# Graph convolution and FFN layer on one core: in the final masked addition, two node tiles of every seven go from VectorE to ScalarE and GpSimd

## The reference

```python
x = x + gnn(layernorm(x), edge_weight, ..., edge_index, ...)   # two graph convolutions and a linear layer
x = x + ffn(layernorm(x)[None], ...)[0]
```

```python
_, idx = jax.lax.top_k(weights, k)
sel_idx = idx[:, :kk]
y = y * w_sel[..., None]
processed = jnp.zeros_like(x).at[batch_idx, sel_idx].set(y)
return processed + x
```

## Time and profile before

| | before |
|---|---|
| time, median of 3 runs | 2256.4 us (2253.57, 2256.4, 2258.93) |
| profiled execution, from its first to its last instruction | 2757.6 us |
| profiled execution, its own time beside the span | not recorded |
| DVE busy | 892.5 us, 32% |
| ACT busy | 994.1 us, 36% |
| POOL busy | 1559.2 us, 57% |
| PE busy | 1849.8 us, 67% |
| mean granted TensorE clock | 0.836 |

### The profile page before, as it was taken

How to read it: one execution, slowest core, us unless ns; L and a number is a source line. 1 busy time by engine, 2 the same in 40 slices (tenths; PEclk the granted TensorE clock), 3 DMA queues, 4 the chain that set the end, 5 groups by cost and what they waited for, 6 DMA issues and landing times.

```text
span 2757.6 us, 44466 instructions
## 1 busy us (share of the span) xinstructions
PE 1849.8 (67%) x7203; PEld 1470.7 (53%) x7204; DVE 892.5 (32%) x2440; ACT 994.1 (36%) x2506; POOL 1559.2 (57%) x1584
## 2 busy tenths in 40 slices
PE   0366666675666565655687787788877777777781
PEld 0255445454444444443476666666666666665671
DVE  6322222222222222221243343333333333333346
ACT  2333333233233333333333443343434344334440
POOL 1556656665665666666455666565666556565600
PEclk9978887877887778777689999988898888888895
DMA  5523323332333333333222222222222222222202
GB/s 173 155 82 90 88 84 88 88 90 84 93 91 86 89 94 91 92 92 90 73 77 78 80 81 82 78 77 76 80 82 82 76 76 82 78 83 80 82 8 93
DMA packets 138002, 237.44 MB, mean 86 GB/s; under 512 B 57535, under 2 KB 87357, under 8 KB 137984
## 3 DMA queue, kind: packets, MB, share of 16 engines
q0 software_dynamic: 75264, 205.62, 26.1%
q1 hardware_dynamic: 47848, 20.06, 2.7%
q10 hardware_dynamic: 14872, 11.58, 1.3%
HBM read 216.94 MB, written 19.38 MB: 86 GB/s over the span
## 4 chain that ended last, share of the span: by engine, by line
PE 29%; issue 21%; another core or an unknown queue 20%; DVEq 11%; DVE 8%; ACT 4%; POOL 3%; ACTq 2%; DMA 2%; POOLq 0%; SPq 0%
PE ps_agg L537 19%; PE ps_dn L628 4%; PE ps_up L635 3%; POOL ring L309 3%; ACT ring L384 2%; DVEq L820 2%; DVEq L808 2%; DVE acc L816 2%; DVEq L816 1%; DVE S L808 1%; DMA ring<-conv_rows,idx_stage 1%; DVEq L838 1%; ACTq L328 1%; DVEq L815 1%
## 5 line engine op out<-in xcount | busy, mean ns | idle before, releaser
L537 PE MATMUL ps_agg<-ring,S 128*128 128x256 f32 x3136 | 974.7, 467 | 719.0 <-ACT ring L384 392.7
L537 PEld LDWEIGHTS ps_agg<-ring,S 128*128 128x128 f32 x3136 | 715.1, 236 | 915.0 <-issue 792.1
L309 POOL DMA_INDIRECT ring<-conv_rows,idx_stage x784 | 774.7, 988 | 535.2 <-DVEq L837 295.4
L309 POOL DMA_INDIRECT ring<-normed_rows,idx_stage x784 | 775.1, 989 | 494.3 <-issue 263.3
L384 ACT ACTIVATE ring<-ring,wc 128x256 f32<-128x256 f32 x1568 | 669.7, 502 | 76.5 <-issue 41.4
L816 DVE TENSOR_TENSOR acc<-acc,ps_agg x490 | 206.3, 421 | 1179.1 <-remote 635.2
L808 DVE TENSOR_TENSOR S<-iota,dstc 128x512 f32 x392 | 271.8, 693 | 484.7 <-issue 480.9
L537 PE MATMUL ps_agg<-ring,S_more 128*128 128x256 f32 x768 | 202.8, 411 | 31.5 <-DVE S_more L808 27.7
L628 PE MATMUL ps_dn<-fw2s,hT 128*128 128x256 f32 x864 | 217.2, 408 | 0.0
L635 PE MATMUL ps_up<-xnT,fw1s 128*128 128x256 f32 x832 | 196.9, 391 | 1.2 <-ACT hT L447 1.2
L537 PEld LDWEIGHTS ps_agg<-ring,S_more 128*128 128x128 f32 x768 | 158.6, 210 | 69.3 <-issue 44.1
(11 more groups left out here) (165 smaller groups left out, 1072.8 us busy)
## 6 DMA issues: line engine op xcount, KB each, us to landing
ring<-normed_rows,idx_stage POOLq DMA_INDIRECT x784
ring<-conv_rows,idx_stage POOLq DMA_INDIRECT x784
conv_rows<-rows ACTq DMA_DIRECT2D x50, 128.0 KB
out_rows<-xs SPq DMA_DIRECT2D x6, 896.0 KB
xs<-in_x SPq DMA_DIRECT2D x4, 1280.0 KB, 14.4
normed_rows<-acc SPq DMA_DIRECT2D x4, 1280.0 KB, 5.2
idx_stage<-idx SPq DMA_DIRECT2D x200, 4.0 KB
normed_rows<-acc SPq DMA_DIRECT2D x1, 1152.0 KB, 4.8
```

Source lines behind the costliest of these rows:

```text
L309: pool.indirect_dma_start(out=ring[:, k, :], out_offset=None, in_=f_dram if l == 0 else t2_dram, in_offset=bass.IndirectOffsetOnAxis(ap=id ...
L537: last = nc.tensor.matmul(to, select[:, t, :], ring[:, q * TG + t, :], start=(t == 0), stop=(t == TG - 1))
```

## The change

In every chunk of seven tiles DVE keeps the first five. For the last two, ACT multiplies `acc` by the column of `mw`, in place, and then POOL adds both products to both `xs` tiles in one instruction of 128 x 512. ACT starts when DVE signals that `mw` is complete (`mask_ready`). POOL waits for ACT's pair (`ffn_scaled`). SP waits for both halves of a chunk before it issues the DMA. DVE's part shrinks from 49 to 35 instructions; ACT gets 14 and POOL 7.

```diff
+        mask_ready, out_ready_pool = sem("mask_ready"), sem("out_ready_pool")
+        ffn_scaled = sem("ffn_scaled")
+        OUT_POOL = 2
...
             for c, (w0, w1) in enumerate(OUTCH):
                 sp.wait_ge(out_ready, c + 1)
+                sp.wait_ge(out_ready_pool, c + 1)
...
+            for c, (w0, w1) in enumerate(OUTCH):
+                pool.wait_ge(ffn_scaled, c + 1)
+                last = nc.gpsimd.tensor_tensor(xs[:, X0 + w1 - OUT_POOL:X0 + w1, :], acc[:, A0 + w1 - OUT_POOL:A0 + w1, :], xs[:, X0 + w1 - OUT_POOL:X0 + w1, :], op=ALU.add)
+                last.then_inc(out_ready_pool, 1)
...
+            act.wait_ge(mask_ready, 1)
+            act.wait_ge(down_kept, NW + SKEW + 1)
+            act.wait_ge(base_done, NW + SKEW + 1)
+            for c, (w0, w1) in enumerate(OUTCH):
+                for w in range(w1 - OUT_POOL, w1):
+                    last = nc.scalar.activation(acc[:, A0 + w, :], acc[:, A0 + w, :], ACT.Copy, scale=mw[:, w:w + 1])
+                last.then_inc(ffn_scaled, 1)
...
             lk(V.tensor_tensor(mw[:, :], mw[:, :], u, op=ALU.mult))
+            dve.sem_inc(mask_ready, 1)
 
             dve.wait_ge(down_kept, NW + SKEW + 1)
             dve.wait_ge(base_done, NW + SKEW + 1)
             for c, (w0, w1) in enumerate(OUTCH):
-                for w in range(w0, w1):
+                for w in range(w0, w1 - OUT_POOL):
```

## The result

Over six runs each, the changed kernel takes 2266.14 us (2265.39 to 2267.36), the kernel before 2257.66 us. The ratio is 1.0037, with a 95% interval of 1.0024 to 1.0050: slower by 8.5 us (5.4 to 11.3). The forecast was slower, 2262.5 us, in a range from 2254.5 to 2269; the narrower range of the forecast's own case, 2258 to 2265.7, just misses the measured time.

What follows compares the result with a forecast made beforehand. DVE's final additions (19.5 us) and the output DMAs (18.9 us) were taken as balanced in the last stage. Alternation delays chunk 1, moving the data's end from 22.8 to 28.9 us: 2256.4 + 6.1 = 2262.5 us, range 2254.5 to 2269.

Steps and rivals of the forecast that it cites:

- the forecast's own case: Last stage: DVE and POOL take turns at the port; +6.1 us, 2262.5 us, with POOL's addition between 0.5 and 1.55 us.
- the alternation of two engines at one read port: Last stage: one POOL addition, then one DVE tile, 1.5 us a pair; +6.1 us; chance 0.53 together with POOL first.
- T0: Start of DVE's first final addition, from which the last stage is counted; 2731.17 us in the profile of the kernel before.
- the sum: Last stage: chunk 1 ready at 11.7 us, 1.05 to first byte, 16.1 of DMA, less 22.8 before: +6.1 us, or 7P - 1.6.
- The term P: Length of one POOL addition of 128 x 512, taken as 1.1 us, with bounds of 0.5 and 1.55 us.
- The gap in front: Ahead of DVE's first final addition: the extra DVE signal, put with SP's second wait below 0.1 us.
- No hold: Last stage, rival: POOL runs beside DVE, which keeps its 0.4 us pace; -0.5 us, 2255.9 us; chance 0.13.
- DVE keeps the port: Last stage, rival: POOL gets in only after DVE's 35 instructions; +12.2 us, 2268.6 us; chance 0.15.
- A part of the addition held: Last stage, rival: POOL holds the port for only part of its addition; with half, +0.6 us, 2257.0 us; chance 0.14.
- its edge of 0.87: Hold in us at which, if the engines alternate, the loss reaches the +4.5 us (0.2%) that counts as slower.
- POOL keeps the port: Last stage, rival: all seven POOL additions go first; +6.9 us, 2263.3 us; counted with the forecast in its 0.53.
- the release and the next start: DVE frees POOL's read 0.13 us before its end, its successor starts 0.085 us before it; so a waiting POOL comes first.

Runs made afterwards that it cites:

- pool_memset: Changed kernel with POOL's addition replaced by a fill with zeros, which reads nothing; time ratio 1.0002 against the kernel before, stage 0.65 us shorter.
- dve_psum: Changed kernel with DVE's last operand a PSUM tile in place of the xs tile; time ratio 0.9999 against the kernel before, stage 0.80 us shorter.
- pool_paced: Changed kernel with POOL's addition of each chunk waiting for DVE's part of the chunk before; time ratio 1.0010 against the kernel before, stage +1.64 us.
- pool_copy: Changed kernel with POOL's addition replaced by a one-input copy of ACT's product to xs; time ratio 0.9992 against the kernel before, stage +0.64 us.
- pool_one: Changed kernel with one tile of seven for ACT and POOL in place of two; time ratio 1.0014 against the kernel before, stage +2.23 us.
- pool_three: Changed kernel with three tiles of seven for ACT and POOL in place of two; time ratio 1.0026 against the kernel before, stage +7.23 us.

## Why the prediction was right

**The direction and the mechanism.** It forecast slower, from the alternation of two engines at one read port. The stretches show three tiles at full pace, then seven pairs, as written. Tile 5 was to be ready at T0 + 4.2: SP issued chunk 0 at T0 + 4.25, which less the 0.17 us of SP before is T0 + 4.1. POOL was to be done at about T0 + 12: it was at T0 + 10.8. The empty DMA stretch between the first and the second chunk is there, up to T0 + 12.1 where the sum had 12.75. pool_memset and dve_psum show the cause from both sides, since the first leaves POOL without a read and the second DVE without its second SBUF input, and the loss becomes a gain of 0.65 and 0.80 us.

**The sizes.** The term P, taken as 1.1 us, was the length of POOL's addition; what counts is the hold, and it measured 1.0. With it the sum is 7 x 1.0 - 1.6 = +5.4 us. The gap in front, which I had put below 0.1 us, was 0.19: DVE's signal and what it puts between L1035 and L1043 in the chain above. The DMA rate, taken as 333 GB/s, was 340 once the chunks were waiting, which makes the 5.37 MB 0.3 us shorter. Together that is 5.4 + 0.2 - 0.3 = +5.3, as measured, in place of +6.1. The closeness of the price was luck, in that two errors met: the addition without a hold is 1.28 us long, not 1.1, and it holds DVE for 1.0 us and not for its whole length, which no row of before could show. With the true length as the price the sum would have been 7 x 1.28 - 1.6 = +7.4 us. The Trainium skill, "GPSIMD Engine Reference", section "Elementwise — side-by-side cycle accounting", led to 1.12 us as an estimate; starts were 1.22 us apart in dve_psum, where DVE did not hold POOL.

**Carrying the profile over.** I carried the difference over unchanged from an execution that was 501 us longer. The changed kernel bears this out: its stage takes 31.97 us in an execution of 2263.2 us and 31.93 in one of 2756.6. For the kernel before it is inferred, since its profiles are all near 2760 us.

**The rivals.** "No hold" gave -0.5 us and was measured, with the hold removed, as -0.65 to -0.80. "DVE keeps the port" would have had POOL's first addition end at T0 + 15; it ended before T0 + 2.5. "A part of the addition held" was true in the small: 1.0 of 1.28 us, which is above its edge of 0.87. "POOL keeps the port" is out too, because each 1.4 us holds one DVE tile. Reading the release and the next start (0.13 us before the end against 0.085) gave the right order; that these two times are the reason for it was not tested.

**What stays open.** The measured +8.5 us has a lower end of 5.4, and the stage explains 5.3. The repeats gave +9.1 and +5.5 us. If there were a cost ahead of the stage, the other kernels with the same added code should show it. Their ratios as us of the kernel before in the same set, less their stage's difference, leave (in us) +1.2 for pool_memset, +1.1 for pool_paced, -2.9 for pool_copy, +0.5 for dve_psum, +1.7 for pool_one and -0.1 for pool_three: a mean of +0.3 us, each uncertain by about 4 us or more. So nothing shows such a cost, but 2 us of it can't be excluded.

## What to carry to other kernels

Before work is moved from VectorE to GpSimd, look at what each of the two reads from SBUF while they overlap. If VectorE's instructions have two SBUF inputs and GpSimd's reads at all, VectorE stands still for a part of GpSimd's instruction, and that hold has to be set against what VectorE saves: 1.00 against 0.8 us for the addition of two tiles, 0.34 against 0.8 for a copy. The sign is visible beforehand in the stretched instructions where the two engines happen to meet. Look also at what the consumer behind them can take: here the output DMAs needed 18.9 us beside DVE's 19.5, so even free help was worth at most 0.8 us. And an engine that runs ahead of need on a shared resource should be paced: one wait took away 3.7 of the 5.3 us. Smaller output chunks, with all of the work left on VectorE, shortened the stage by 1.15 us.

## What the runs showed of the hardware

- The hold is not the whole of the holding instruction. A GpSimd addition of 512 columns takes 1.28 us where neither engine holds the other (dve_psum) and holds VectorE for 1.00; a copy of 512 columns holds it for 0.34; a fill holds it not at all. The Trainium skill, "SBUF — State Buffer", section "Who interferes with whom", calls the shared pair of ports an exclusive lock and says, in its item on VectorE's two-port modes, that whoever issues first has the pair for the whole instruction. Which instructions contend is in these runs as it says; the hold between an instruction with two SBUF inputs and a GpSimd read is shorter than the recorded instruction.
- With both queues full the engines went strictly in turn: one tile of VectorE's, one addition of GpSimd's, seven times, 1.4 us for each pair.
- The same kernel took 2257.7, 2765.8, 2814.0 and 2757.3 us in the four sets of runs; for the last three the chip is recorded, and each was another. The last stage took 26.6 to 26.7 us in each of its three profiles, of 2757.6 to 2762.7 us. The changed kernel was profiled at both speeds, and there the difference lies in the two passes over the edges: from the first indirect DMA to the last they take 2050 us in the execution of 2263.2 us (81.9 to 2131.5) and 2536 us in that of 2756.6 us (82.0 to 2617.5), which is 486 of the 493 us. Whether the chip or something else sets it was not tried.
